# Two attention groups summed side by side in one PSUM bank, and turned once for both

## The chip, the cores and the metric

The kernel runs on one core of a Trainium2 chip. The metric is the device time of one execution in microseconds (us). The engines are TensorE (PE in the rows, its weight loads PEld), VectorE (DVE), ScalarE (ACT), GpSimd (POOL) and SyncE (SP), which issues most DMAs.

## The reference

One "macaron" layer on x of shape (8, 512, 128), all in float32: half a step of a feed-forward part that holds an attention of its own and a mixture of 8 experts, then an attention with rotary positions and 4 key and value heads, then the feed-forward part again. Both attentions have 16 heads of 8 elements.

```python
def _msa(x, w_qkv, w_proj):                      # 512 tokens of a batch as 4 x 128 here
    attn = softmax(q @ k.T / sqrt(8)); y = attn @ v; return y @ w_proj
def _L0_ffn_ref(x, ...):
    x = x + _msa(_layernorm(x, ln1_w, ln1_b), w_qkv, w_proj)
    return x + _moe_mlp(_layernorm(x, ln2_w, ln2_b), gate_w, gate_b, w1, w2)   # best expert of 8 per token
x = x + 0.5 * _L0_ffn_ref(_layernorm(x), ...)
x = x + _L0_attn_ref(_layernorm(x), w_q, w_k, w_v, w_o)
x = x + 0.5 * _L0_ffn_ref(_layernorm(x), ...)
```

The abridged lines leave out shapes. In the kernel each of the 8 batches of 512 tokens attends within itself.

## The kernel before

**Stages.** The program is two streams of attention, each followed by blocks of experts. Stream 0 (label 0) takes the 8 batches of the first feed-forward part. Stream 1 (label 1) takes 16: 8 of the middle attention and 8 of the second feed-forward part. A batch has 16 heads, worked on in G = 4 groups of J = 4 heads. So there are 32 groups in stream 0 and 64 in stream 1, 96 in all; n counts them within a stream.

**One group.** Group n takes four steps, kt = 0 to 3, one for each 128 keys. In a step TensorE computes the scores of 4 heads against 128 keys with all 512 queries (`score`, L839), ScalarE writes their exponentials to SBUF (L1181, four tiles of 128x512 per step), and TensorE multiplies them with the values (`weigh`, L851), one step later. Softmax needs a maximum for each query beforehand: in the same step TensorE also computes scores the other way round for group n + 2 (`max_score`, L823, four of 64x512), and VectorE reduces each two of them to maxima (`take_max`, L1210, two per step). The maxima of a group are split in two parts (L1218, L1220), turned (`turn_max`, L830), copied (L1232) and sent by DMA into rows of Q.

A step has two halves on TensorE. Each half is two matmuls of L823, two of L839 and eight of L851 (four heads, each float32 matmul as two instructions). `weigh` gives each head its own 32 partitions of bank 7: rows 32j to 32j + 8 hold 8 sums of values and, from a column of ones in V, the sum of the exponentials (V1 = 9).

**After a group.** ScalarE copies the whole bank 7 to the tile outT (`copy_out`, L1038) in step (n + 1, 0). TensorE turns it with four 128x128 transposes (`turn_out`, L860) in the list of step (n + 1, 2). VectorE takes the reciprocal of 16 sums per token (L1242) and multiplies (L1245) into the rows N (`normalise`).

**The ring.** L823 and everything else that isn't scores or weighted sums (rows of maxima, turned outputs, projections, values, gates) write to a ring of four PSUM banks. A use of the ring takes as many slots as it has banks; `put` rounds a list of a step up to an even number by making the last entry two slots wide. A slot can be used again when its consumer, VectorE or ScalarE, has released the use four slots back (`bank_for`). The lists stand in `Plan.group`: at kt = 0 the rows of maxima, at kt = 2 the turned output, and with either what `Plan.slot` adds. At kt = 2 that is q for n = 0 modulo 4, v for 2, proj for 3 and, for 1, k (middle attention), gate (feed-forward) or nothing. Of the 48 steps (n, 2) with odd n, 22 have "out" and proj, 12 "out" and gate, 6 "out" and k, and 8 "out" alone (n = 1, 3, 5 of stream 0; n = 3, 25, 29, 33, 37 of stream 1).

**Other places.** The tile V holds three slots of values; `copy_v` (L1071, L1075) fills one per batch, 24 in all. The tile `empty` holds zero rows with token numbers that name spare rows of `by_token`; eight of its entries are written behind each expert's tokens (`write_tails`), the other eight as two loads of 8 x 128 rows at the end of `sorted_x`. `later_loads` is a list of which SyncE issues one per group in stream 0.

Of the kernel before, what the change touches and what calls it, by code (L numbers as in the profile page):

```python
# [21 lines left out]
U32 = mybir.dt.uint32  # L22
# [4 lines left out]
P = 128  # L27
# [20 lines left out]
VCOLS = G * QT * J * V1  # L48
# [129 lines left out]
def setup(nc, c, a):  # L178
    with ExitStack() as ctx:
# [18 lines left out]
        def _(pool):  # L198
# [10 lines left out]
            nc.gpsimd.iota(c.empty[:, :, D].bitcast(U32), pattern=[[P, 2 * E]], base=NT * P, channel_multiplier=1)  # L209
# [37 lines left out]
def later_loads(c, a):  # L247

    loads = [(c.w1[:, e * HID:(e + 1) * HID], a["w1"][e]) for e in range(E)]
    loads += [(cols(c.w2, e * HID, HID).rearrange("p (k n) -> p k n", k=HT), a["w2"][e].rearrange("(k p) n -> p k n", p=P))  # L250
              for e in range(E)]
    loads += [
        (c.sorted_x[(E + (E + 1) * half) * REGION:(E + (E + 1) * half) * REGION + E * P, :].rearrange("(u p) w -> p u w", p=P),
         c.empty[:, E:2 * E, :]) for half in range(HALVES)]
    loads += [
        (c.wqk_mid[:, :], a["w_qk_mid"]), (c.wqk_rot[:, :], a["w_qk_rot"]),
        (c.wv[:, :], a["w_v"]), (c.wo[:, :], a["w_o"]),
        (c.cos[:, :], a["cos"]), (c.sin[:, :], a["sin"]),
    ]
    return loads  # L260

# [15 lines left out]
class Plan:  # L277
# [108 lines left out]
def stream(nc, c, ctx, a, label, kinds, past, blocks):  # L386
# [6 lines left out]
    if True:  # L393
# [7 lines left out]
        v4 = c.V[:, :].rearrange("p (b k g j e) -> p b k g j e", b=VSLOTS, k=QT, g=G, j=J)  # L401
# [151 lines left out]
        def write_tails(eng, half, experts):  # L553

            eng.wait_ge(s.tabled, half + 1)
            for expert in experts:
# [5 lines left out]
        def sync(sp):  # L562
# [60 lines left out]
            def main():  # L623
# [4 lines left out]
                for n in range(last):  # L628
# [33 lines left out]
        def gpsimd(pool):  # L662
# [145 lines left out]
        def tensor(pe):  # L808
# [47 lines left out]
            def turn_out(n):  # L856
                bank = bank_for("out", n)
                pe.wait_ge(s.out_copied, n + 1)
# [170 lines left out]
        def scalar(act):  # L1029
# [4 lines left out]
            def copy_out(n):  # L1034
                act.wait_ge(s.pv, 4 * n + 4)
                if n:
                    filled(act, "out", n - 1)
# [28 lines left out]
            def copy_v(b, bank):  # L1066
# [3 lines left out]
                if plan.ffn(b):  # L1070
                    ins = nc.scalar.activation(v.rearrange("p (h e) -> p h e", e=V1)[:, :, 0:HD],  # L1071
                                               bank.rearrange("p (h d) -> p h d", d=HD), ACT.Copy)
                else:
                    h = QT * G
                    ins = nc.scalar.activation(v.rearrange("p (h j e) -> p h j e", h=h, j=J)[:, :, :, 0:HD],  # L1075
                                               bank[:, 0:h * HD].rearrange("p (h j d) -> p h j d", h=h, j=1)
                                               .broadcast_to((P, h, J, HD)), ACT.Copy)
# [88 lines left out]
            def main():  # L1166
# [8 lines left out]
                for n in range(last):  # L1175
                    for kt in range(QT):
# [6 lines left out]
                        if kt == 0 and n:  # L1183
# [14 lines left out]
        def vector(dve):  # L1198
# [39 lines left out]
            def normalise(n):  # L1238
                filled(dve, "out", n)
                turned = ring[turns["out", n].first % RING].rearrange("p (t j r) -> p t j r", t=QT, j=J)  # L1240
                rec = cols(c.recip, n % 2 * QT * J, QT * J).rearrange("p (t j) -> p t j", t=QT)
                nc.vector.reciprocal(rec, turned[:, :, :, HD]).then_inc(s.recip, 1)  # L1242
                dve.wait_ge(s.recip, n + 1)
                dst = outputs(n // G).rearrange("p t (g j d) -> p t g j d", g=G, j=J)[:, :, n % G, :, :]
                freed(nc.vector.tensor_tensor(dst, turned[:, :, :, 0:HD],  # L1245
                                              rec.rearrange("p t (j o) -> p t j o", o=1).broadcast_to((P, QT, J, HD)),
                                              ALU.mult), "out", n)
# [429 lines left out]
def build(nc, a, out):  # L1677
    with ExitStack() as ctx:
# [9 lines left out]
        c.rest, c.zeroed = ctx.enter_context(nc.semaphore("rest")), ctx.enter_context(nc.semaphore("zeroed"))  # L1688
        c.X, c.Y, c.N = sb("X", [P, B * S]), sb("Y", [P, B * S]), sb("N", [P, NT * W])
# [20 lines left out]
        c.recip = sb("recip", [P, 2 * QT * J])  # L1710
        c.logits, c.onehot, c.rank = sb("logits", [P, 2 * QT * E]), sb("onehot", [P, 2 * QT * E]), sb("rank", [P, 2 * RANKS])
        c.before, c.empty, c.temp = sb("before", [P, HALVES * (HT_ROWS + 1) * E]), sb("empty", [P, 2 * E, W]), [sb(f"temp{i}", [P, 100]) for i in range(2)]
# [108 lines left out]
```

## Time and profile before

| | us |
|---|---|
| median of three runs | 1563.21 |
| lowest and highest run | 1561.63, 1566.58 |
| the profiled execution | 1566.45 |
| its span, first to last instruction | 1564.7 |
| TensorE busy | 1406.8 |
| VectorE busy | 1185.5 |
| ScalarE busy | 1124.5 |

The profiled execution has 1.75 us around its span. Its stretches: stream 0 attends from about 66 to 467 us and stream 1 from about 631 to 1436 us; the rest is the opening and the experts. Busy shares are those of whole stretches; what waits for what is read from the timeline of one group.

### The profile page before, as it was taken

The page shows a single profiled execution, that of the slowest core. Times are in us where ns is not written, and L with a number is a line of the kernel's source. Part 1 is how long each engine was busy: PE and PEld are TensorE (multiplying, and loading weights), DVE is VectorE, ACT ScalarE, POOL GpSimd, SP SyncE. Part 2 cuts the span into 40 slices and gives each one's busy share as a digit, 9 for nine tenths or more (in the row PEclk, how much of TensorE's full clock was granted, in tenths as well). Part 3 has the DMA queues.
Part 4 walks back from the last instruction along what each step waited for, and adds up shares of the span by engine and source line. Part 5 has one row for each costly group of instructions (what it writes and reads, how often), then busy time and mean ns, then how long its engine had stood idle before and what let it go on. Part 6 is the DMA issues. An engine that isn't in the chain of part 4 may idle for free.

```text
span 1564.7 us, 35538 instructions
## 1 busy us (share of the span) xinstructions
PE 1406.8 (90%) x12228; PEld 687.4 (44%) x12228; DVE 1185.5 (76%) x1945; ACT 1124.5 (72%) x2148; POOL 639.8 (41%) x972
## 2 busy tenths in 40 slices
PE   2899999999999886999999999999999999999895
PEld 1333334333339773333333333333334343334885
DVE  5788888888855254888888888888888888894532
ACT  1478887788785452778888887888887878787553
POOL 2422344542226555333544453233324543213753
PEclk8699999999999986999999999999999999999998
DMA  4344333533102315323322333332333233211243
GB/s 119 95 111 114 103 100 108 132 94 95 47 26 60 105 49 154 96 77 93 94 80 68 98 95 101 93 82 67 93 94 82 73 99 99 60 38 37 72 113 104
DMA packets 101423, 137.60 MB, mean 88 GB/s; under 512 B 29664, under 2 KB 72032, under 8 KB 101248
## 3 DMA queue, kind: packets, MB, share of 16 engines
q1 hardware_dynamic: 70864, 85.82, 19.1%
q0 software_dynamic: 24000, 45.04, 12.0%
q10 hardware_dynamic: 6384, 4.47, 1.0%
q8 instruction: 102, 1.67, 0.4%
q14 instruction: 73, 0.60, 0.1%
HBM read 79.05 MB, written 53.51 MB: 85 GB/s over the span
## 4 chain that ended last, share of the span: by engine, by line
PE 55%; DVE 31%; issue 6%; POOL 2%; DMA 2%; SPq 2%; ACT 1%; DVEq 0%; ACTq 0%; POOLq 0%
DVE maxima L1210 26%; PE banks L851 14%; PE banks L839 11%; PE banks L823 11%; PE banks L878 3%; PE banks L1554 3%; PE banks L860 3%; PE banks L1563 3%; PE banks L904 1%; PE banks L885 1%; SPq L463 1%; POOL by_token L1537 1%; DVE stats L1287 1%; DVE split L1218 1%; POOL sorted_x L691 1%
## 5 line engine op out<-in xcount | busy, mean ns | idle before, releaser
L1210 DVE TENSOR_REDUCE maxima<-banks 128x2 f32<-128x1024 f32 x768 | 924.2, 1222 | 171.9 <-PE banks L823 166.8
L1181 ACT ACTIVATE work<-banks 128x512 f32<-128x512 f32 x1536 | 829.3, 597 | 149.2 <-PE banks L839 135.2
L823 PE MATMUL banks<-K,Q 64*128 64x512 f32 x1536 | 572.7, 463 | 56.3 <-DVE maxima L1210 36.4
L839 PE MATMUL banks<-Q,K 64*128 64x512 f32 x1536 | 567.7, 451 | 0.6
L851 PE MATMUL banks<-work,V 128*9 128x256 f32 x6144 | 476.8, 382 | 1.6 <-ACT work L1181 0.8
L823 PEld LDWEIGHTS banks<-K,Q 64*128 64x128 f32 x1536 | 229.9, 190 | 214.6 <-DVE maxima L1210 126.4
L839 PEld LDWEIGHTS banks<-Q,K 64*128 64x128 f32 x1536 | 229.3, 186 | 181.7 <-issue 137.4
L851 PEld LDWEIGHTS banks<-work,V 128*9 128x9 f32 x6144 | 91.5, 88 | 276.1 <-issue 204.5
L710 POOL TENSOR_TENSOR lo<-full,hi 128x512 fp32r<-128x512 f32 x42 | 53.7, 1278 | 251.7 <-ACT hi L1059 144.4
L1617 DVE COPY work<-w 128x512 f32 x88 | 43.7, 497 | 87.2 <-PE banks L1554 75.5
L1563 PE MATMUL banks<-w,work 128*128 x736 | 102.3, 284 | 2.5 <-issue 1.3
L1537 POOL DMA_INDIRECT by_token<-work x76 | 76.2, 1003 | 66.2 <-ACT work L1597 55.6
L1554 PE MATMUL banks<-work 128*128 128x128 f32 x704 | 97.6, 284 | 0.6 <-DVE work L1617 0.6
L1563 PEld LDWEIGHTS banks<-w,work 128*128 128x128 f32 x736 | 94.3, 200 | 3.4 <-issue 3.3
L1554 PEld LDWEIGHTS banks<-work 128*128 128x128 f32 x704 | 89.9, 200 | 3.3 <-issue 2.0
L138 POOL TENSOR_SCALAR root<-moments 128x4 f32<-128x4 f32 x38 | 8.9, 233 | 196.8 <-DVE moments L1294 158.6
L1592 ACT ACTIVATE work<-banks 128x512 f32<-128x512 f32 x92 | 54.8, 596 | 30.6 <-PE banks L1554 30.5
L691 POOL DMA_INDIRECT sorted_x<-N,pos x64 | 65.2, 1019 | 19.9 <-issue 11.0
L860 PE MATMUL banks<-ident,outT 128*128 128x128 f32 x384 | 62.8, 286 | 6.2 <-DVE maxima L1210 4.6
L1057 ACT ACTIVATE full<-banks 128x512 f32<-128x512 f32 x46 | 27.5, 597 | 52.7 <-PE banks L878 51.9
L542 POOL TENSOR_TENSOR full<-full,cos_sb 128x512 f32<-128x512 f32 x12 | 15.4, 1286 | 119.9 <-ACT swap L1053 119.8
L1587 ACT ACTIVATE work<-banks,ln 128x128 f32<-128x128 f32 x92 | 41.8, 455 | 31.1 <-PE banks L1547 24.7
(187 smaller groups left out, 1331.8 us busy)
## 6 DMA issues: line engine op xcount, KB each, us to landing
Q<-q_scratch SPq DMA_DIRECT2D x188, 128.0 KB, 2.6
K<-k_scratch SPq DMA_DIRECT2D x376, 64.0 KB, 2.4
Q<-zero_rows SPq DMA_DIRECT2D x182, 64.0 KB, 2.2
q_scratch<-hi POOLq DMA_DIRECT2D x42, 256.0 KB, 4.7
q_scratch<-lo POOLq DMA_DIRECT2D x42, 256.0 KB, 6.8
k_scratch<-hi POOLq DMA_DIRECT2D x21, 256.0 KB, 4.6
k_scratch<-lo POOLq DMA_DIRECT2D x21, 256.0 KB, 6.8
work<-sorted_x SPq DMA_DIRECT2D x76, 66.0 KB, 1.9
```

The lines of the kernel that those rows point to most:

```text
L691: nc.gpsimd.indirect_dma_start(c.sorted_x[:, :], bass.IndirectOffsetOnAxis(ap=c.pos[:, t:t + 1], axis=0), c.rows[:, t, :], None).then_inc( ...
L710: nc.gpsimd.tensor_tensor(lo(b)[i].bitcast(F32R), full(b)[i], hi(b)[i], ALU.subtract).then_inc(s.lo[i], 1)
L823: fill(nc.tensor.matmul(bank, q4[parts(j), n % SLOTS, j // 2, qt * P:(qt + 1) * P], k4[parts(j), n % SLOTS, j // 2, :], start=True, stop=T ...
L839: nc.tensor.matmul(scp[x % EXPS][:, :], k4[parts(j), n % SLOTS, j // 2, kt * P:(kt + 1) * P], q4[parts(j), n % SLOTS, j // 2, :], start=Tr ...
L851: ins = nc.tensor.matmul(outp[32 * j:32 * j + V1, q], v4[:, n // G % VSLOTS, kt, n % G, j, :], prob[:, kt, j, q], start=(kt == 0 and half ...
L860: ins = nc.tensor.transpose(bank[:, t * P:(t + 1) * P], c.outT[:, t * P:(t + 1) * P], c.ident[:, :])
L1181: nc.scalar.activation(prob[:, kt, j ^ 1, :], scp[x % EXPS][:, :], ACT.Exp, scale=SCALE).then_inc(s.probs, 1)
L1210: nc.vector.tensor_reduce(c.maxima[:, at:at + 9:8], c.banks[:, k * S:(k + 2) * S].rearrange("p (m n) -> p m n", m=2), AX.X, ALU.max).then_ ...
L1537: nc.gpsimd.indirect_dma_start(c.by_token[:, :], bass.IndirectOffsetOnAxis(ap=x_sb(i)[:, D:D + 1].bitcast(U32), axis=0), y_sb[i % ring], N ...
L1554: ins = nc.tensor.matmul(hp[i % 2][:, t * P:(t + 1) * P], w1(i)[:, t * P:(t + 1) * P], uT[i % 2], start=True, stop=True)
L1563: ins = nc.tensor.matmul(yp, h[i % 2][:, t * P:(t + 1) * P], cols(c.w2, at + t * D, D), start=(t == 0), stop=(t == HT - 1))
L1592: nc.scalar.activation(h[i % 2], hp[i % 2][:, :], ACT.Gelu_apprx_tanh).then_inc(s.gelu, 1)
```

## The change

The results of an even group n and the odd group n + 1 now lie side by side in the same 32 partitions of bank 7. V gets 27 columns per pair and head: 9 of the even group (8 values and a one), 9 zeros, 9 of the odd group. An even group's weights are columns 0 to 17, an odd group's columns 9 to 26, so each `weigh` matmul has 18 stationary columns for 9, and each adds zeros to the other group's sums. The accumulation starts at the even group's first matmul and stops at the odd group's last. `copy_out`, `turn_out` and `normalise` run once per pair, for "out" of odd n alone; `normalise` takes one reciprocal of 32 sums and makes two multiplications. `copy_v` becomes two activations of half the size.

For room, `empty` is halved: first it holds the names for the two large spare loads, which SyncE issues together at n = 1 (`spare_rows`); at n = 8 GpSimd waits for them and writes the other names, for which `write_tails` waits.

```diff
@@ VCOLS
-VCOLS = G * QT * J * V1
+VPAIR = 3 * V1
+VCOLS = QT * G // 2 * J * VPAIR
@@ setup
-            nc.gpsimd.iota(c.empty[:, :, D].bitcast(U32), pattern=[[P, 2 * E]], base=NT * P, channel_multiplier=1)
+            nc.gpsimd.iota(c.empty[:, :, D].bitcast(U32), pattern=[[P, E]], base=NT * P + E * P, channel_multiplier=1)
@@ Plan.group
-        if kt == 2 and 1 <= n <= self.last:
+        if kt == 2 and 2 <= n <= self.last and n % 2 == 0:
             names += [("out", n - 1)]
@@ sync main
+                    if n == 1 and later:
+                        spare_rows(sp, c)
@@ gpsimd opening
-                    nc.gpsimd.memset(c.V[:, :], 1.0).then_inc(c.v_clear, 1)
+                    link(nc.gpsimd.memset(c.V[:, :], 1.0))
+                    nc.gpsimd.memset(c.V[:, :].rearrange("p (x e) -> p x e", e=VPAIR)[:, :, V1:2 * V1], 0.0).then_inc(c.v_clear, 1)
@@ gpsimd main
+                    if label == 0 and n == 2 * G:
+                        pool.wait_ge(c.spare, 16 * HALVES)
+                        nc.gpsimd.iota(c.empty[:, :, D].bitcast(U32), pattern=[[P, E]], base=NT * P, channel_multiplier=1)\
+                            .then_inc(c.renamed, 1)
@@ weigh
-                    if kt == 0:
-                        wait(pe, s.out_copied, n)
+                    if kt == 0 and n % 2 == 0:
+                        wait(pe, s.out_copied, n // 2)
...
+                odd = n % 2
                 for j in range(J):
-                    ins = nc.tensor.matmul(outp[32 * j:32 * j + V1, q], v4[:, n // G % VSLOTS, kt, n % G, j, :], prob[:, kt, j, q],
-                                           start=(kt == 0 and half == 0), stop=(kt == QT - 1 and half == 1))
+                    ins = nc.tensor.matmul(outp[32 * j:32 * j + 2 * V1, q],
+                                           v4[:, n // G % VSLOTS, kt, n % G // 2, j, V1 * odd:V1 * odd + 2 * V1], prob[:, kt, j, q],
+                                           start=(n % 2 == 0 and kt == 0 and half == 0), stop=(n % 2 == 1 and kt == QT - 1 and half == 1))
@@ scalar: copy_v, main
+                pairs_of = v.rearrange("p (h j e) -> p h j e", h=QT * G // 2, j=J)
+                for odd in range(2):
+                    dst = pairs_of[:, :, :, 2 * V1 * odd:2 * V1 * odd + HD]
...
+                    ins = nc.scalar.activation(dst, src, ACT.Copy)
...
-                        if kt == 0 and n:
+                        if kt == 0 and n and n % 2 == 0:
                             copy_out(n - 1)
@@ normalise
-                nc.vector.reciprocal(rec, turned[:, :, :, HD]).then_inc(s.recip, 1)
+                nc.vector.reciprocal(rec, turned[:, :, :, HD:2 * V1:V1]).then_inc(s.recip, 1)
...
+                for odd in range(2):
+                    ins = nc.vector.tensor_tensor(dst[:, :, n % G - 1 + odd, :, :], turned[:, :, :, V1 * odd:V1 * odd + HD],
+                                                  rec[:, :, :, odd:odd + 1].broadcast_to((P, QT, J, HD)), ALU.mult)
```

On TensorE, step (7, 2) of stream 0, the first with proj, reads so before (work is the tile of exponentials; a count behind x is of heads or tiles):

```order
L839 MATMUL banks<-Q,K 128x512
L823 MATMUL banks<-K,Q 128x512
L851 MATMUL banks<-work,V 9x256 x4
L860 MATMUL banks<-ident,outT 128x128 x4
L904 MATMUL banks<-wproj,turned 128x128 x4
L823 MATMUL banks<-K,Q 128x512
L839 MATMUL banks<-Q,K 128x512
```

and so after the change, with the new file's line numbers (L836 and L852 for L823 and L839, L865 for L851, L919 for L904):

```order
L852 MATMUL banks<-Q,K 128x512
L836 MATMUL banks<-K,Q 128x512
L865 MATMUL banks<-work,V 18x256 x4
L919 MATMUL banks<-wproj,turned 128x128 x4
L836 MATMUL banks<-K,Q 128x512
L852 MATMUL banks<-Q,K 128x512
```

The four transposes are gone from this odd step, proj keeps its place, and the stationary operand of the weighted sums has 18 columns. In steps (n, 2) with even n the transposes stay.

On VectorE, steps (7, 2) and (8, 2) of stream 0 read so before:

```order
L1210 TENSOR_REDUCE maxima<-banks 128x2 x2
L1242 RECIPROCAL recip<-banks 128x16
L1245 TENSOR_TENSOR N<-banks,recip 128x4x32
L1210 TENSOR_REDUCE maxima<-banks 128x2 x2
...
L1210 TENSOR_REDUCE maxima<-banks 128x2 x2
L1242 RECIPROCAL recip<-banks 128x16
L1245 TENSOR_TENSOR N<-banks,recip 128x4x32
L1210 TENSOR_REDUCE maxima<-banks 128x2 x2
L1218 CAST split<-maxima 128x2x8
```

and step (8, 2) so after:

```order
L1226 TENSOR_REDUCE maxima<-banks 128x2 x2
L1258 RECIPROCAL recip<-banks 128x32
L1262 TENSOR_TENSOR N<-banks,recip 128x4x32 x2
L1226 TENSOR_REDUCE maxima<-banks 128x2 x2
L1234 CAST split<-maxima 128x2x8
```

The odd step has no reciprocal and no multiplication any more; the even step has one more multiplication.

## Rows read from the trace of the kernel before

**Rows 1.** The page's first part: busy time, share of the span, instructions of each engine.

```profile
PE 1406.8 (90%) x12228; PEld 687.4 (44%) x12228; DVE 1185.5 (76%) x1945; ACT 1124.5 (72%) x2148; POOL 639.8 (41%) x972
```

**Rows 2.** Stream 1's stretch: busy PE, PEld, DVE, ACT, POOL; granted clock, DMA share, GB/s.

```profile
640.00:1435.00 795.00, 756.84 (x6844) 303.90 (x6842) 674.79 (x1010) 646.25 (x1201) 311.05 (x475) 1.00 0.31 82
```

**Rows 3.** Timeline of TensorE at an odd step with proj: start and duration in us.

```profile
1229.98 0.62 PE L851 MATMUL banks<-work,V 128*9 128x256 f32 x8
...
1231.19 0.62 PE L851 MATMUL banks<-work,V 128*9 128x256 f32 x8
1231.74 0.66 PE L860 MATMUL banks<-ident,outT 128*128 128x128 f32 x4
1232.24 1.06 PE L904 MATMUL banks<-wproj,turned 128*128 128x128 f32 x8
...
1233.88 0.62 PE L851 MATMUL banks<-work,V 128*9 128x256 f32 x8
```

**Rows 4.** Timeline of VectorE over the same step; in brackets its idle time before.

```profile
1230.23 2.40 DVE L1210 TENSOR_REDUCE maxima<-banks 128x2 f32<-128x1024 f32 x2
...
1234.06 2.48 DVE L1210 TENSOR_REDUCE maxima<-banks 128x2 f32<-128x1024 f32 x2 [0.94 <-PE banks L823]
```

**Rows 5.** Timeline of TensorE at an odd step whose list is "out" alone.

```profile
1001.50 0.62 PE L851 MATMUL banks<-work,V 128*9 128x256 f32 x8
1002.05 0.66 PE L860 MATMUL banks<-ident,outT 128*128 128x128 f32 x4
1003.00 0.49 PE L823 MATMUL banks<-K,Q 64*128 64x512 f32 x1 [0.28 <-DVE maxima L1210]
...
1003.66 0.62 PE L851 MATMUL banks<-work,V 128*9 128x256 f32 x8
```

**Rows 6.** Timeline of VectorE over that same step.

```profile
998.05 4.89 DVE L1210 TENSOR_REDUCE maxima<-banks 128x2 f32<-128x1024 f32 x4 [0.71 <-PE banks L823]
1002.86 0.25 DVE L1242 RECIPROCAL recip<-banks 128x16 f32<-128x16 f32 x1
1003.21 0.29 DVE L1245 TENSOR_TENSOR N<-banks,recip 128x128 f32<-128x128 f32 x1
1003.84 2.47 DVE L1210 TENSOR_REDUCE maxima<-banks 128x2 f32<-128x1024 f32 x2 [0.34 <-PE banks L823]
```

**Rows 7.** Timeline of TensorE at a kt = 0 step with rows of maxima.

```profile
1225.86 0.27 PE L830 MATMUL banks<-ident,split 128*32 128x128 f32 x1 [0.88 <-DVE maxima L1210]
```

**Rows 8.** Timeline of weight loads at another odd step with proj.

```profile
314.13 0.12 PEld L851 LDWEIGHTS banks<-work,V 128*9 128x9 f32 x8 [0.36 <-issue]
314.68 0.42 PEld L860 LDWEIGHTS banks<-ident,outT 128*128 128x128 f32 x4 [0.43 <-DVE maxima L1210]
315.07 0.97 PEld L904 LDWEIGHTS banks<-wproj,turned 128*128 128x128 f32 x8
```

**Rows 9.** Timeline of VectorE at two even steps, ahead of kt = 3.

```profile
1220.90 2.47 DVE L1210 TENSOR_REDUCE maxima<-banks 128x2 f32<-128x1024 f32 x2 [0.55 <-PE banks L823]
...
1246.86 1.23 DVE L1210 TENSOR_REDUCE maxima<-banks 128x2 f32<-128x1024 f32 x1 [0.72 <-PE banks L823]
```

**Rows 10.** Groups by line: count, then busy us, mean ns of one, idle before.

```profile
L851 PEld LDWEIGHTS banks<-work,V 128*9 128x9 f32 x6144 | 91.5, 88 | 276.1 <-issue 204.5 <-ACT work L1181 71.2
...
L1597 ACT ACTIVATE work<-banks 128x128 f32<-128x128 f32 x92 | 25.5, 277 | 32.2 <-PE banks L1563 31.9
...
L830 PEld LDWEIGHTS banks<-ident,split 128*32 128x32 f32 x96 | 9.1, 95 | 75.7 <-issue 70.9 <-DVE split L1220 4.8
...
L1071 ACT ACTIVATE V<-banks 128x512 f32<-128x512 f32 x16 | 9.6, 599 | 20.4 <-PE banks L885 19.7 <-issue 0.6
```

**Rows 11.** Timeline of the opening, GpSimd and VectorE.

```profile
1.33 1.86 POOL L205 MEMSET empty<- 128x2112 f32 x1
...
7.11 2.95 DVE L1402 TENSOR_SCALAR root<-moments 128x4 f32<-128x4 f32 x1
9.97 1.56 POOL L730 MEMSET V<- 128x1728 f32 x1
```

More of the change, by code:

```diff
@@ L252, in later_loads @@
     loads += [
-        (c.sorted_x[(E + (E + 1) * half) * REGION:(E + (E + 1) * half) * REGION + E * P, :].rearrange("(u p) w -> p u w", p=P),
-         c.empty[:, E:2 * E, :]) for half in range(HALVES)]
-    loads += [
         (c.wqk_mid[:, :], a["w_qk_mid"]), (c.wqk_rot[:, :], a["w_qk_rot"]),
@@ L260, in later_loads, with spare_rows @@
     return loads
+def spare_rows(sp, c):
+    for half in range(HALVES):
+        at = (E + (E + 1) * half) * REGION
+        sp.dma_start(c.sorted_x[at:at + E * P, :].rearrange("(u p) w -> p u w", p=P), c.empty[:, :, :]).then_inc(c.spare, 16)
 def load_outputs(eng, c, b):
@@ L555, in write_tails @@
             eng.wait_ge(s.tabled, half + 1)
+            eng.wait_ge(c.renamed, 1)
             for expert in experts:
@@ L857, in turn_out @@
                 bank = bank_for("out", n)
-                pe.wait_ge(s.out_copied, n + 1)
+                pe.wait_ge(s.out_copied, n // 2 + 1)
                 for t in range(QT):
@@ L1035, in copy_out @@
                 act.wait_ge(s.pv, 4 * n + 4)
-                if n:
-                    filled(act, "out", n - 1)
+                if n > 1:
+                    filled(act, "out", n - 2)
                 nc.scalar.activation(c.outT[:, :], outp[:, :], ACT.Copy).then_inc(s.out_copied, 1)
@@ L1069, in copy_v @@
                 v = cols(c.V, b % VSLOTS * VCOLS, VCOLS)
[L1070 to L1077, printed above, removed]
+                pairs_of = v.rearrange("p (h j e) -> p h j e", h=QT * G // 2, j=J)
+                for odd in range(2):
+                    dst = pairs_of[:, :, :, 2 * V1 * odd:2 * V1 * odd + HD]
+                    if plan.ffn(b):
+                        src = bank.rearrange("p (h o j d) -> p h o j d", o=2, j=J, d=HD)[:, :, odd, :, :]
+                    else:
+                        src = bank[:, 0:QT * G * HD].rearrange("p (h o j d) -> p h o j d", o=2, j=1, d=HD)[:, :, odd, :, :]\
+                            .broadcast_to((P, QT * G // 2, J, HD))
+                    ins = nc.scalar.activation(dst, src, ACT.Copy)
                 evacuated(ins, "v", b)
@@ L1240, in normalise @@
                 turned = ring[turns["out", n].first % RING].rearrange("p (t j r) -> p t j r", t=QT, j=J)
-                rec = cols(c.recip, n % 2 * QT * J, QT * J).rearrange("p (t j) -> p t j", t=QT)
-                nc.vector.reciprocal(rec, turned[:, :, :, HD]).then_inc(s.recip, 1)
[L1243 to L1247, printed above, removed]
+                rec = cols(c.recip, n // 2 % 2 * 2 * QT * J, 2 * QT * J).rearrange("p (t j o) -> p t j o", t=QT, j=J)
+                nc.vector.reciprocal(rec, turned[:, :, :, HD:2 * V1:V1]).then_inc(s.recip, 1)
+                dve.wait_ge(s.recip, n // 2 + 1)
+                dst = outputs(n // G).rearrange("p t (g j d) -> p t g j d", g=G, j=J)
+                for odd in range(2):
+                    ins = nc.vector.tensor_tensor(dst[:, :, n % G - 1 + odd, :, :], turned[:, :, :, V1 * odd:V1 * odd + HD],
+                                                  rec[:, :, :, odd:odd + 1].broadcast_to((P, QT, J, HD)), ALU.mult)
+                freed(ins, "out", n)
             def add_gate_bias(f):
@@ L1688, in build @@
         c.rest, c.zeroed = ctx.enter_context(nc.semaphore("rest")), ctx.enter_context(nc.semaphore("zeroed"))
+        c.spare, c.renamed = ctx.enter_context(nc.semaphore("spare")), ctx.enter_context(nc.semaphore("renamed"))
         c.X, c.Y, c.N = sb("X", [P, B * S]), sb("Y", [P, B * S]), sb("N", [P, NT * W])
@@ L1709, in build @@
         c.warm = sb("warm", [P, 1])
-        c.recip = sb("recip", [P, 2 * QT * J])
+        c.recip = sb("recip", [P, 4 * QT * J])
         c.logits, c.onehot, c.rank = sb("logits", [P, 2 * QT * E]), sb("onehot", [P, 2 * QT * E]), sb("rank", [P, 2 * RANKS])
-        c.before, c.empty, c.temp = sb("before", [P, HALVES * (HT_ROWS + 1) * E]), sb("empty", [P, 2 * E, W]), [sb(f"temp{i}", [P, 100]) for i in range(2)]
+        c.before, c.empty, c.temp = sb("before", [P, HALVES * (HT_ROWS + 1) * E]), sb("empty", [P, E, W]), [sb(f"temp{i}", [P, 100]) for i in range(2)]
         c.pos, c.expert_at, c.row_at = sb("pos", [P, NT], U32), sb("expert_at", [1, HALVES * NBLK], U32), sb("row_at", [1, HALVES * NBLK], U32)
```

2 lines of the change are left out of this document (1 added, 1 removed).

## The prediction

> **What bounds the kernel now.** I read the page first, for who is busy: TensorE 90% of the span, VectorE 76%, ScalarE 72% [rows 1]. In stream 1's stretch TensorE is busy 756.84 of 795 us at a granted clock of 1.00, that is 2.4 GHz, VectorE 674.79 [rows 2]. Shares so close don't tell who sets the time, so I read the timelines of single steps.
>
> In the odd step with proj, the eight `weigh` matmuls of one half start at 1229.98 and those of the next at 1231.19: a half-step is 1.21 us when nothing stands between. The next start is 1233.88, so the transposes and proj stretch 1.21 to 2.69 us [rows 3]. Over this place VectorE ends its reductions at 1230.23 + 2.40 = 1232.63, normalises, and then sits idle 0.94 us until TensorE has filled two banks [rows 4]. TensorE's own work sets the time here.
>
> In the odd step with "out" alone, the `weigh` starts lie 2.16 us apart (1001.50 to 1003.66), and TensorE restarts at 1003.00 after an idle wait for VectorE [rows 5]. The four reductions of kt = 1 and 2 end at 998.05 + 4.89 = 1002.94; at once TensorE restarts [rows 6]. So with the ring's two slots taken by "out", the next L823 needs the banks of the last reduction: this step is closed by VectorE, and then VectorE waits 0.34 us for the fill. The two engines stop for each other once at kt = 2 and once at kt = 0, where TensorE waits 0.88 us for a reduction before it can turn the maxima [rows 7]. Between these places (kt = 1 to 2, and kt = 3 to 0) VectorE reduces without a gap.
>
> **The change part by part.**
>
> *Transposes, 40 odd steps with another entry (22 proj, 12 gate, 6 k).* The loads of the four transposes start at 314.68 and proj's at 315.07 [rows 8]: 0.39 us by which all behind comes earlier. Is TensorE still the one waited for? It began its next pair about 0.66 us (1003.66 - 1003.00, from rows 5) before the `weigh` at 1233.88, at 1233.22; 0.39 earlier is 1232.83, still behind the end of the reductions at 1232.63 [rows 4]. VectorE also loses its 0.25 + 0.29 us of reciprocal and multiplication [rows 6], so it waits at least as before. 40 x 0.39 = 15.6 us. The most a step with proj could give before VectorE closes it is 2.69 - 2.16 = 0.53 us.
>
> *The 8 odd steps with "out" alone.* Here the two ring slots go as well. TensorE can run on at 1002.05, and has the next two banks filled 0.84 us later (1003.00 to 1003.84 is that delay), at 1002.89. VectorE, without normalising, is free at 1002.94 rather than restarting at 1003.84 [rows 5, 6]: 0.90 us each, 7.2 us.
>
> *The even steps.* TensorE does what it did. VectorE has a second multiplication, 0.29 us [rows 6] and some 0.04 of gap. It is covered by the idle time ahead of the reduction of kt = 3, which is 0.55 us in the step with v (behind statistics too) and 0.72 with q [rows 9]. Zero; without this cover it would be 48 x 0.33 = 16 us. The reciprocal of 32 for 16 I take as no longer.
>
> *ScalarE's 48 copies of bank 7 fall away.* They stand in steps where TensorE waits for VectorE [rows 7], so I give them nothing. Nobody else is queued on them: an odd group's `weigh` no longer waits for a copy, but it did not wait before either, with the start-to-start at 1.21.
>
> *Eighteen columns for nine.* No row shows this load. The eight loads of a half take 0.12 us together, though one takes 88 ns [rows 8, 10], so they start within about 32 ns of each other and overlap. From below: a load of 32 columns takes 95 ns [rows 10], that is (95 - 88)/23 = 0.3 ns per column, 2.7 ns for nine. From above: four loads of 128 columns take 0.42 us [rows 8], 105 ns each, 0.82 ns per column, or 7.4 ns for nine; if all eight were paid one behind another, 59 ns in a half-step. I take one load of 7.4 ns exposed per half-step, since the eight overlap in the row. It counts only where TensorE is the one waited for: four of a group's eight half-steps (kt = 1 and 2; from kt = 3 to kt = 0 TensorE has the 0.88 us to spare), 384 in all: 384 x 0.0074 = 2.8 us. The stream of 256 queries is unchanged.
>
> The Trainium skill, "TensorE: Matmul & The Clock Gate", section "LDWEIGHTS (loading the stationary operand)", puts a load at columns / 1.2 ns, here 7.5 ns more, and its Part 3 says that loads overlap running matmuls only in another row group; all eight here use the same 128 rows. Taken together that would make eight loads of nine columns 60 ns end to end, where the row shows starts within about 32 ns, so it is only partly borne out; by it the sum would lose about 23 us, which is the rival below.
>
> *Values.* 24 copies of 599 ns become pairs of 256 elements each; between 277 ns for 128 elements and 599 for 512 [rows 10] that is 0.38 each, 0.17 us more per batch. ScalarE begins its exponentials later by that; a part may reach TensorE through the score banks. Bounds are 0 and 24 x 0.17 = 4.1; I take 1.0.
>
> *Opening.* Half of the 1.86 us memset of `empty` goes, so all behind the setup comes 0.93 earlier. The memset of V, 1.56 us, becomes 2.34 and gets a second one of half the size, 0.78. VectorE's L1402 took 2.95 us and ended at 10.06, when the next GpSimd memset had begun [rows 11]; a later one of its kind could now be held in the same way for up to about 0.8 us. Together zero, within 0.9 either way.
>
> *Spare rows.* Two loads move to n = 1, ahead of SyncE's weight load, and one wait and one iota enter GpSimd's queue at n = 8. Behind SyncE's issues stand the maxima's rows for a group a whole group's time ahead, and behind GpSimd's wait the k and q of a batch two groups ahead. Zero; 1 us at most.
>
> **Sum.** -15.6 - 7.2 + 2.8 + 1.0 = -19.0 us on the profiled execution's 1566.45, so 1547.4. That execution was 3.2 us above the median of three, 1563.21; against the median it is 1544.2, which I forecast as 1544.
>
> **Rivals.**
>
> *Weight loads eat the gain (1563).* If the eight loads follow one another, each of the 384 half-steps grows by 59 ns: 22.7 us against 22.8 saved, and 1 for V. For it: all eight share their rows, and loads of 128 columns do start 105 ns apart. Against it: eight loads fit in 0.12 us. The TensorE page of the skill speaks for this one, as said.
>
> *Loads are paid in every half-step, slower (1586).* The same 59 ns, but with no cover at kt = 3 and 0 either: 768 x 0.059 = 45.3 us, less 22.8, is +22.5. It decides from 22.8/768 = 30 ns per half-step on, if each one pays. Against it: 4 x 0.059 = 0.24 us is less than the 0.88 us that TensorE waits there [rows 7].
>
> *VectorE takes over (1554).* If something late on VectorE (choices of experts, statistics) closes the odd steps, half of each 0.39 is lost, 7.8 us, and perhaps 2 of the even steps' multiplications: about -9. For it: only 0.20 us lie between 1232.63 and 1232.83. Against it: it has 0.94 us idle afterwards.
>
> *More gain (1534).* The drained start of proj may hide less than 0.39 suggests: with 0.53 in each of the 40, and no price for loads or values, 21.2 + 7.2 = 28.4 us.
>
> **How the numbers follow.** My forecast (between 1537 and 1551) 0.66; weight loads eat the gain, in whole or in large part (1552 to 1565) 0.13; VectorE takes over 0.09; more gain 0.06; slower 0.06. The range reaches from 1536, inside the larger gain, to 1558, inside the weight-load case, leaving about 2 in 10 outside. A measurement of this kernel tells about 0.3%, 4.7 us, from no change. Faster: forecast, larger gain, VectorE case and some of the weight-load case, 0.85; the same 0.09; slower 0.06.
>
> **What would show it.** Transposes, copies of bank 7 and reciprocals must be 192, 48 and 48. The odd step with proj should go from 2.69 to about 2.31 us between `weigh` starts, the lone one from 2.16 to about 1.22. A plain half-step tells the weight load: 1.21 to 1.22 by me, 1.27 by the rival. VectorE's idle time ahead of kt = 3 should fall to about 0.2 and 0.4 us in even steps, and stay above zero. If the half-step is 1.22 and the time still doesn't fall, the gain went to VectorE, which would show as TensorE idle for L1210 in the odd steps with proj.

## The result, and the profile after

The changed kernel takes 1546.47 us (median of four runs, 1546.29 to 1549.42) against 1562.55 of the kernel before (four runs): the ratio is 0.9893, 95% interval 0.9875 to 0.9911. The forecast was 1544 us, range 1536 to 1558. In a later comparison (the run again below), where the kernel before took 1577.32 us, the ratio was 0.9887 (0.9864 to 0.9910). The profiled execution went from 1566.45 to 1546.33 us, 20.1 us less, against 19.0 worked out for it.

The page's first part for the changed kernel [of before: rows 1]:

```profile
PE 1391.6 (90%) x12036; PEld 680.1 (44%) x12036; DVE 1177.6 (76%) x1897; ACT 1102.3 (71%) x2124; POOL 640.9 (41%) x974
```

TensorE has 192 matmuls and VectorE 48 instructions fewer; the shares stay within a point of what they were. In stream 1's stretch, now 622 to 1414 us [rows 2]; the columns are busy us of TensorE, its weight loads, VectorE, ScalarE and GpSimd, then the granted clock, DMA share and GB/s:

```profile
622.00:1414.00 792.00, 756.55 (x6800) 302.61 (x6796) 677.73 (x988) 637.51 (x1196) 311.76 (x476) 1.00 0.32 84
```

The clock is 2.4 GHz (1.00) in both. The odd step with proj on TensorE [rows 3], here of group 51 (line numbers are the new file's: L865 weighs, L919 is proj, L836 the scores for maxima):

```profile
1260.68 0.63 PE L865 MATMUL banks<-work,V 128*18 128x256 f32 x8
...
1261.90 0.63 PE L865 MATMUL banks<-work,V 128*18 128x256 f32 x8
...
1263.12 0.63 PE L865 MATMUL banks<-work,V 128*18 128x256 f32 x8
1263.67 1.16 PE L919 MATMUL banks<-wproj,turned 128*128 128x128 f32 x8
...
1265.42 0.63 PE L865 MATMUL banks<-work,V 128*18 128x256 f32 x8
```

Half-steps are 1.22 us now, and from 1263.12 to 1265.42 it takes 2.30 us where it took 2.69. VectorE in the same step [rows 4]:

```profile
1262.13 2.43 DVE L1226 TENSOR_REDUCE maxima<-banks 128x2 f32<-128x1024 f32 x2
1265.60 1.23 DVE L1226 TENSOR_REDUCE maxima<-banks 128x2 f32<-128x1024 f32 x1 [1.05 <-PE banks L836]
```

Its idle time has grown from 0.94 to 1.05 us: TensorE is still the one waited for. A step with "out" alone before, now with an empty list (group 29) [rows 5]:

```profile
982.84 0.63 PE L865 MATMUL banks<-work,V 128*18 128x256 f32 x8
...
984.06 0.63 PE L865 MATMUL banks<-work,V 128*18 128x256 f32 x8
...
985.28 0.63 PE L865 MATMUL banks<-work,V 128*18 128x256 f32 x8
...
986.50 0.63 PE L865 MATMUL banks<-work,V 128*18 128x256 f32 x8
987.06 0.50 PE L836 MATMUL banks<-K,Q 64*128 64x512 f32 x1
...
987.72 0.63 PE L865 MATMUL banks<-work,V 128*18 128x256 f32 x8
```

Nothing stands between the half-steps any more: 986.50 to 987.72 is 1.22 us for 2.16. VectorE [rows 6]:

```profile
983.01 7.36 DVE L1226 TENSOR_REDUCE maxima<-banks 128x2 f32<-128x1024 f32 x6 [0.71 <-PE banks L836]
```

Six reductions follow each other where there were four, a pause and two. In an even step VectorE has the longer normalisation ahead of kt = 3 [rows 9]:

```profile
1199.86 0.35 DVE L1258 RECIPROCAL recip<-banks 128x32 f32<-128x32 f32 x1
1200.24 0.49 DVE L1262 TENSOR_TENSOR N<-banks,recip 128x128 f32<-128x128 f32 x2
1200.65 0.48 DVE L1304 BATCH_NORM_STATS2 stats<-X 128x6 f32<-128x128 f32 x2
1201.39 2.48 DVE L1226 TENSOR_REDUCE maxima<-banks 128x2 f32<-128x1024 f32 x2 [0.27 <-PE banks L836]
```

Idle time fell from 0.55 to 0.27 us and hides it. The groups by line: count, busy us, mean ns of one, idle before [rows 10]:

```profile
L865 PEld LDWEIGHTS banks<-work,V 128*18 128x18 f32 x6144 | 103.5, 96 | 275.2 <-issue 200.5 <-ACT work L1197 74.3
...
L875 PE MATMUL banks<-ident,outT 128*128 128x128 f32 x192 | 31.3, 286 | 5.9 <-DVE maxima L1226 4.3 <-ACT outT L1053 1.6
L1053 ACT ACTIVATE outT<-banks 128x512 f32<-128x512 f32 x48 | 29.1, 606 | 2.4 <-PE banks L865 2.4
...
L1258 DVE RECIPROCAL recip<-banks 128x32 f32<-128x32 f32 x48 | 16.7, 348 | 12.2 <-PE banks L875 12.2
...
L1093 ACT ACTIVATE V<-banks 128x256 f32<-128x256 f32 x48 | 16.4, 400 | 27.6 <-PE banks L900 27.6
```

192 transposes, 48 copies of the bank and 48 reciprocals, as the change says. The reciprocal of 32 takes 348 ns, where that of 16 took 247 (0.25 in the timeline [rows 6]). A value copy takes 400 ns.

**Where the time went.** The attention stretches can be taken out of the trace by the first and last half-step of `weigh` of each stream. Each row is worked out from four start times of one profiled execution.

| kernel | first `weigh` at | stream 0 | between | stream 1 | rest | both streams |
|---|---|---|---|---|---|---|
| before | 66.7 | 400.1 | 164.4 | 804.8 | 128.7 | 1204.9 |
| changed | 65.3 | 392.2 | 164.2 | 792.1 | 130.8 | 1184.3 |
| changed, later comparison | 66.0 | 394.4 | 168.1 | 793.7 | 134.5 | 1188.1 |

The gain lies in the streams, 20.6 us. What lies between and behind them is the experts, whose length differs by some us from one profiled execution to the next (158.0 to 164.4 us between the streams in the traces of before, changed and experiments 1, 2, 3 and 5), whether changed or not. The changed kernel and its three variants of experiment 5 show it: their spans lie 5.9 us apart (1538.7 to 1544.6 us), their streams 1.6 (1183.7 to 1185.3). So below both are given: the ratio of all runs, and the sum of the two streams in the trace.

The start times of all 768 half-steps tell more. From the kernel before to the changed one, the 40 odd steps with another entry are 15.3 us shorter in all and the 8 lone ones 7.5 us. Of the other half-steps 13 differ by over 0.1 us each, together by -1.0 (0.9 of it at the very first); all the rest, which differ by less than that, are 3.1 us longer in sum. That is the price of the wider loads as the streams show it, and no further cost stands out.

### The profile page after: what moved, and what is told of

Its sections match the earlier page's. It is cut to its first block, busy times and chain, and to the rows that moved or that the text cites. A ratio compares the mean times of both kernels' runs of the same rounds, so it can differ in the third digit from the quotient of the medians.

```text
span 1544.6 us, 34941 instructions
## 1 busy us (share of the span) xinstructions
PE 1391.6 (90%) x12036; PEld 680.1 (44%) x12036; DVE 1177.6 (76%) x1897; ACT 1102.3 (71%) x2124; POOL 640.9 (41%) x974
## 4 chain that ended last, share of the span: by engine, by line
PE 57%; DVE 27%; issue 7%; DMA 3%; SPq 2%; POOL 2%; ACT 1%; DVEq 0%; ACTq 0%; POOLq 0%
DVE maxima L1226 23%; PE banks L865 16%; PE banks L852 12%; PE banks L836 11%; PE banks L893 4%; PE banks L1571 3%; PE banks L1580 3%; PE banks L875 2%; PE banks L919 2%; PE banks L900 1%; SPq L468 1%; POOL by_token L1554 1%; PE banks L935 1%; DVE stats L1304 1%; POOL sorted_x L699 1%
## 5 line engine op out<-in xcount | busy, mean ns | idle before, releaser
L836 PE MATMUL banks<-K,Q 64*128 64x512 f32 x1536 | 571.8, 463 | 51.2 <-DVE maxima L1226 34.4
L852 PE MATMUL banks<-Q,K 64*128 64x512 f32 x1536 | 567.3, 451 | 0.5
L865 PE MATMUL banks<-work,V 128*18 128x256 f32 x6144 | 482.3, 386 | 1.5 <-ACT work L1197 0.8
L836 PEld LDWEIGHTS banks<-K,Q 64*128 64x128 f32 x1536 | 229.6, 190 | 209.4 <-DVE maxima L1226 130.8
L852 PEld LDWEIGHTS banks<-Q,K 64*128 64x128 f32 x1536 | 229.3, 186 | 178.0 <-ACT work L1197 132.1
L865 PEld LDWEIGHTS banks<-work,V 128*18 128x18 f32 x6144 | 103.5, 96 | 275.2 <-issue 200.5
L1554 POOL DMA_INDIRECT by_token<-work x76 | 76.9, 1012 | 67.7 <-ACT work L1614 57.4
L140 POOL TENSOR_TENSOR rstd<-root,minus_half 128x4 f32<-128x4 f32 x52 | 54.1, 1040 | 4.4
```

The lines of the kernel that those rows point to most:

```text
L140: link(eng.tensor_tensor(out, half, c.minus_half[:, :], ALU.pow))
L836: fill(nc.tensor.matmul(bank, q4[parts(j), n % SLOTS, j // 2, qt * P:(qt + 1) * P], k4[parts(j), n % SLOTS, j // 2, :], start=True, stop=T ...
L852: nc.tensor.matmul(scp[x % EXPS][:, :], k4[parts(j), n % SLOTS, j // 2, kt * P:(kt + 1) * P], q4[parts(j), n % SLOTS, j // 2, :], start=Tr ...
L865: ins = nc.tensor.matmul(outp[32 * j:32 * j + 2 * V1, q], v4[:, n // G % VSLOTS, kt, n % G // 2, j, V1 * odd:V1 * odd + 2 * V1], prob[:, k ...
L1554: nc.gpsimd.indirect_dma_start(c.by_token[:, :], bass.IndirectOffsetOnAxis(ap=x_sb(i)[:, D:D + 1].bitcast(U32), axis=0), y_sb[i % ring], N ...
```

## The experiments

Every ratio is taken against the kernel before, run beside it. "Both streams" is the sum of the two attention stretches in one trace, as above.

**1. Wider loads alone (w18, w28).** The kernel before, with 18 or 28 columns in each weighted sum; the extra sums are never read. WIDE is 18 or 28.

```diff
+VSTRIDE = VCOLS + WIDE - V1
...
-                    ins = nc.tensor.matmul(outp[32 * j:32 * j + V1, q], v4[:, n // G % VSLOTS, kt, n % G, j, :], prob[:, kt, j, q],
+                    at = n // G % VSLOTS * VSTRIDE + ((kt * G + n % G) * J + j) * V1
+                    ins = nc.tensor.matmul(outp[32 * j:32 * j + WIDE, q], c.V[:, at:at + WIDE], prob[:, kt, j, q],
```

> The kernel before, with 18 stationary columns in each weighted-sum matmul (the nine columns of the next head are taken along; their sums are never read) and nothing else changed. In the trace of the changed kernel a plain half-step went from 1.21 to 1.22 us. Theory: only the four half-steps per group pay in which TensorE is the one waited for: 384 x 0.009 = about +3.3 us on the kernel before. Rival: every half-step pays, 768 x 0.009 = +6.7 us. Rival of the prediction, eight loads one behind another: half-steps of 1.27 us and +23 us or more.

> The same with 28 columns, as a larger dose: 19 more than nine. If a half-step grows in proportion to the columns, by about 0.95 ns for each, it is 1.23 us. Theory (four of eight half-steps pay): +7 us on the kernel before. Rival (all pay): +14 us. If the load's price is a fixed step and not per column, it is the same as with 18 columns.

With 18 columns: ratio 1.0015 (1.0002 to 1.0028), both streams 1209.3 us, 4.4 more. With 28: ratio 1.0046 (1.0030 to 1.0061), 1212.5 us, 7.6 more. The timeline of TensorE with 28 columns, at kt = 1 and 2 of group 29:

```profile
1002.34 0.64 PE L853 MATMUL banks<-work,V 128*28 128x256 f32 x8
...
1003.57 0.64 PE L853 MATMUL banks<-work,V 128*28 128x256 f32 x8
...
1004.79 0.64 PE L853 MATMUL banks<-work,V 128*28 128x256 f32 x8
...
1006.02 0.64 PE L853 MATMUL banks<-work,V 128*28 128x256 f32 x8
```

and the group of its loads:

```profile
L853 PEld LDWEIGHTS banks<-work,V 128*28 128x28 f32 x6144 | 116.6, 105 | 275.9 <-issue 204.8 <-ACT work L1183 70.7
```

Three half-steps of a run last 3.63 us with nine columns (997.87 to 1001.50, of which rows 5 show the last), 3.66 with 18 (982.84 to 986.50 above), and 3.68 with 28 (1002.34 to 1006.02). Over all plain half-steps the mean is 1.212, 1.221 (1.220 in the changed kernel) and 1.229 us, so 0.9 ns for each added column: it goes by columns and is paid about once per half-step, not eight times. A half-step of 1.27 us is ruled out. That not all of them are on the path is shown by 28 columns: 1.0046 is 7.2 us, interval 4.7 to 9.5, where 384 x 0.017 = 6.5 and 768 x 0.017 = 13. With 18 columns, 2.4 us (0.3 to 4.4) fits 384 x 0.0085 = 3.3 and leaves out 6.5.

The streams' 4.4 and 7.6 look like more than half. But 1.5 of the 4.4 stands at one place, group 3 of stream 0, and 1.4 of the 7.6 at nine single half-steps that differ by over 0.1 us each. Without these the streams are 2.9 and 6.1 us longer, close to 384 half-steps in both. Every plain half-step grows, and those with TensorE's wait for VectorE at kt = 0 shrink, by 1.8 us in all with 18 columns and 3.5 with 28: there the covered part is given back.

The measured 0.9 ns is near the 0.82 per column at which loads of 128 columns follow each other [rows 8]. The Trainium skill, "TensorE: Matmul & The Clock Gate", section "LDWEIGHTS (loading the stationary operand)", has columns / 1.2 ns for a load, 0.83 ns per column. The measured 0.9 agrees with one such load exposed per half-step. In Part 3 of that page the Trainium skill says that loads overlap running matmuls only in another row group; read as "loads of the same rows follow one another", this does not describe these eight.

**2. Pairing without wider loads (narrow).** The odd group's sums are added onto the even group's rows and both multiplications read that place, so the output is not the layer's.

```diff
-                    ins = nc.tensor.matmul(outp[32 * j:32 * j + 2 * V1, q],
-                                           v4[:, n // G % VSLOTS, kt, n % G // 2, j, V1 * odd:V1 * odd + 2 * V1], prob[:, kt, j, q],
+                    ins = nc.tensor.matmul(outp[32 * j:32 * j + V1, q],
+                                           v4[:, n // G % VSLOTS, kt, n % G // 2, j, 2 * V1 * odd:2 * V1 * odd + V1], prob[:, kt, j, q],
...
-                nc.vector.reciprocal(rec, turned[:, :, :, HD:2 * V1:V1]).then_inc(s.recip, 1)
+                nc.vector.reciprocal(rec, turned[:, :, :, HD:HD + 1].broadcast_to((P, QT, J, 2))).then_inc(s.recip, 1)
```

> The changed kernel with nine stationary columns again: the odd group's sums are added onto the even group's in the same rows and both multiplications read that one place as before, so the output is not the reference's. It shows what pairing gives without the wider loads. Theory: about 3.3 us under the changed kernel, near 20 us under the kernel before, with half-steps of 1.21 us. Rival (all half-steps pay): 6.7 us under the changed kernel.

Ratio 0.9851 (0.9833 to 0.9868), 1540.64 us; both streams 1182.5 us, 1.8 less than the changed kernel's. By the ratio it is 0.0042 or 6.6 us less against the first comparison of the changed kernel, and 5.6 against the later one, whose interval overlaps. So this run doesn't tell 3.3 from 6.7; the half-steps are 1.212 us again.

**3. The ring slots of the lone steps (hold).** In the eight odd steps whose list the change emptied, two slots are taken by one small transpose.

```diff
+        if kt == 2 and 1 <= n < self.last and not names:
+            names += [("hold", n)]
...
+                bank = bank_for("hold", n)
+                fill(nc.tensor.transpose(bank[0:32, 0:P], c.ident[:, 0:32], c.ident[:, :]), "hold", n)
...
+                        freed(nc.vector.tensor_copy(c.held[:, :], ring[turns["hold", i].first % RING][0:32, 0:4]), "hold", i)
```

> The changed kernel, but in the steps kt = 2 whose list is now empty (the eight lone odd steps) two ring slots are taken up by one small transpose of 32 columns and a tiny copy on VectorE. Theory: the slots, not the four transposes, closed these steps: the start-to-start of the weighted sums goes back from 1.22 to about 2.15 us, and the time is some 7 us above the changed kernel. Rival: the transposes' own time was the cost; then the small one costs about 0.1 to 0.3 us each, 1 to 2 us in all.

Ratio 0.9922 (0.9903 to 0.9940); both streams 1192.7 us, 8.4 more than the changed kernel's, 7.5 of it in the eight steps themselves. TensorE at group 29:

```profile
988.60 0.63 PE L867 MATMUL banks<-work,V 128*18 128x256 f32 x8
989.15 0.29 PE L882 MATMUL banks<-ident 128*32 128x128 f32 x1
990.09 0.50 PE L838 MATMUL banks<-K,Q 64*128 64x512 f32 x1 [0.65 <-DVE held L1295]
...
990.75 0.63 PE L867 MATMUL banks<-work,V 128*18 128x256 f32 x8
```

VectorE at the same place:

```profile
985.11 4.92 DVE L1234 TENSOR_REDUCE maxima<-banks 128x2 f32<-128x1024 f32 x4 [0.71 <-PE banks L838]
989.95 0.14 DVE L1295 COPY held<-banks 32x4 f32<-32x4 f32 x1
990.93 1.23 DVE L1234 TENSOR_REDUCE maxima<-banks 128x2 f32<-128x1024 f32 x1 [0.84 <-PE banks L838]
```

One transpose of 0.29 us in place of four, and the `weigh` starts are 2.15 us apart again (988.60 to 990.75), because TensorE waits 0.65 us for VectorE: its four reductions end at 985.11 + 4.92 = 990.03. The slots closed these steps, as forecast; the transposes' length there didn't matter.

**4. TensorE's work put back in all 48 odd steps (peback).** VectorE's and ScalarE's part of the saving stays.

```diff
+        if kt == 2 and 1 <= n < self.last and n % 2:
+            names += [("hold", n)]
...
+                for t in range(QT):
+                    ins = nc.tensor.transpose(bank[:, t * P:(t + 1) * P], c.ident[:, :], c.ident[:, :])
+                fill(ins, "hold", n)
```

> The changed kernel with TensorE's work and the ring slots of the odd steps put back: four transposes of the identity in each of 48 odd steps kt = 2, and a tiny copy on VectorE that releases the bank. VectorE's reciprocals and multiplications, and ScalarE's copies, stay away. Theory: all of the gain was TensorE's 0.39 us in 40 steps and the closing of 8; so the attention stretches go back to those of the kernel before with 18 columns (1209 us), and the time is about 1.001 of the kernel before. Rival: what VectorE and ScalarE no longer do is part of the gain; then the time stays some us under the kernel before.

Ratio 1.0051 (1.0035 to 1.0067). Both streams 1211.3 us, 23.2 more than the changed kernel's in the same comparison (1188.1), where 22.8 were forecast for the odd steps. The step with proj on TensorE:

```profile
1241.24 0.63 PE L867 MATMUL banks<-work,V 128*18 128x256 f32 x8
1241.80 0.66 PE L883 MATMUL banks<-ident 128*128 128x128 f32 x4
1242.29 1.06 PE L927 MATMUL banks<-wproj,turned 128*128 128x128 f32 x8
...
1243.94 0.63 PE L867 MATMUL banks<-work,V 128*18 128x256 f32 x8
```

It is 2.70 us long again. The 40 steps give back 15.6 us and the 8 lone ones 7.5; all other half-steps together differ by 0.1. So no part of the gain in the streams is left for VectorE's or ScalarE's saving.

The total missed what was expected: about 1.001, where the interval starts at 1.0035. Of the 26.8 us between the profiled executions of peback and the changed kernel beside it, 3.6 lie outside the streams, most of it between and behind them, where this edit adds nothing. The ratio is 0.0036 (5.6 us) above that of w18, whose TensorE does the same in the streams; that kernel ran in the earlier comparison, and its streams are 2.0 us shorter. What makes the rest was not settled.

**5. Engines beside the path (mul3, copies, setup).** One more multiplication per normalisation, 46 copies of 128x512 back on ScalarE (the expectation counts 47; the first odd group of each stream has none), and GpSimd's memset at its old length.

```diff
+                    if odd == 0:
+                        nc.vector.tensor_tensor(c.spill[:, :].rearrange("p (t j d) -> p t j d", t=QT, j=J), turned[:, :, :, 0:HD],
+                                                rec[:, :, :, 0:1].broadcast_to((P, QT, J, HD)), ALU.mult)
```

```diff
+                        if kt == 0 and n % 2 and n > 1:
+                            act.wait_ge(s.pv, 4 * n)
+                            act.wait_ge(s.out_copied, n // 2)
+                            filled(act, "out", n - 2)
+                            nc.scalar.activation(c.outT[:, :], c.outT[:, :], ACT.Copy).then_inc(s.idled, 1)
```

```diff
             nc.gpsimd.memset(c.empty[:, :, :], 0.0)
+            nc.gpsimd.memset(c.Y[:, 0:E * W], 0.0)
```

> The changed kernel with one more multiplication (128x128 into a tile that nobody reads) in each of the 48 normalisations, some 0.33 us of VectorE each. In the changed kernel VectorE is idle ahead of kt = 3 for about 0.43 to 0.62 us in steps with q, 0.18 to 0.27 in steps with v, 0.11 in the few with the output alone. Theory: the idle time covers it but for what is lacking in the steps with v and the lone ones: about +3 us on the changed kernel. Rival (VectorE sets the time of the even steps): 48 x 0.33 = +16 us. It also tells that the second multiplication of the change, which met more idle time, cost nothing.

> The changed kernel with a copy of 128x512 put back on ScalarE in 47 of the odd steps kt = 0 (outT onto itself, where the copy of the bank stood before). Theory: these copies lie beside a wait of TensorE for VectorE; the time is that of the changed kernel within 1 us. Rival: the copies were part of the gain; up to 47 x 0.6 = 28 us, and at least some us above the changed kernel.

> The changed kernel with the setup's memset on GpSimd at its old length (a second one of 1056 elements per partition on a tile that is written later anyway). Theory: the setup ends 0.9 us later and so do the first reductions, +0.9 us. Rival: the opening is bound by something else and nothing moves.

| kernel | ratio | interval | both streams |
|---|---|---|---|
| mul3 | 0.9876 | 0.9854 to 0.9898 | 1185.3 |
| copies | 0.9868 | 0.9845 to 0.9891 | 1185.0 |
| setup | 0.9887 | 0.9867 to 0.9908 | 1183.7 |

All three are the changed kernel's time (0.9893 and 0.9887) within their intervals. mul3 was expected at +3 and shows +1.0 in the streams, where copies shows +0.7 and setup -0.6: no more than such traces differ. VectorE in mul3's step with v:

```profile
1200.17 0.35 DVE L1258 RECIPROCAL recip<-banks 128x32 f32<-128x32 f32 x1
1200.55 0.29 DVE L1262 TENSOR_TENSOR N<-banks,recip 128x128 f32<-128x128 f32 x1
1200.76 0.28 DVE L1265 TENSOR_TENSOR spill<-banks,recip 128x128 f32<-128x128 f32 x1
1200.96 0.28 DVE L1262 TENSOR_TENSOR N<-banks,recip 128x128 f32<-128x128 f32 x1
1201.16 0.47 DVE L1307 BATCH_NORM_STATS2 stats<-X 128x6 f32<-128x128 f32 x2
1201.69 2.48 DVE L1226 TENSOR_REDUCE maxima<-banks 128x2 f32<-128x1024 f32 x2
```

The added multiplication starts only 0.21 us (1200.55 to 1200.76, 1200.96) after the one before, and so uses up the idle time and no more. The rivals, 16 us and 28 us, are ruled out. The setup's 0.9 us can't be told from the spread of the totals; the first `weigh` came at 67.2 rather than 65.3, but with mul3, whose opening is unchanged, it came at 67.7, so the opening itself varies by more. Its early part did move. VectorE's small L1420 in setup (L1419 in the changed kernel, whose rows stand further down):

```profile
7.13 2.95 DVE L1420 TENSOR_SCALAR root<-moments 128x4 f32<-128x4 f32 x1
...
12.48 0.74 DVE L1420 TENSOR_SCALAR root<-rstd 128x4 f32<-128x4 f32 x1
```

The second ends at 13.22 rather than 12.53, 0.69 us later. Whether that reaches the end of the program isn't shown.

**6. Nine columns where they do (mixed), and the changed kernel again.**

```diff
+                many = V1 if odd == 0 and kt else 2 * V1
                 for j in range(J):
-                    ins = nc.tensor.matmul(outp[32 * j:32 * j + 2 * V1, q],
-                                           v4[:, n // G % VSLOTS, kt, n % G // 2, j, V1 * odd:V1 * odd + 2 * V1], prob[:, kt, j, q],
+                    ins = nc.tensor.matmul(outp[32 * j:32 * j + many, q],
+                                           v4[:, n // G % VSLOTS, kt, n % G // 2, j, V1 * odd:V1 * odd + many], prob[:, kt, j, q],
```

> The changed kernel once more, on the chip and beside the runs that the next two are compared with. Theory: near 1546 us, 0.989 of the kernel before; the two attention stretches together near 1184.3 us in its trace, as in the first one, and what differs lies between the streams and at the end.

> The changed kernel with nine stationary columns in the even groups' matmuls of kt = 1 to 3, where the zeros add nothing that is needed; kt = 0 keeps 18, which writes the odd group's rows. Correct, and three of eight half-steps a pair have the narrow load. Theory: these half-steps fall from 1.220 to 1.212 us, some 1 to 2 us on the whole, under what a measurement tells; the trace shows it. Rival: changing the number of columns between matmuls costs something, and the half-steps don't fall or grow.

The changed kernel: 0.9887 (0.9864 to 0.9910), both streams 1188.1. mixed: 0.9869 (0.9845 to 0.9893), both streams 1186.2, 1.9 less. TensorE in mixed:

```profile
1002.77 0.63 PE L866 MATMUL banks<-work,V 128*18 128x256 f32 x8
...
1003.99 0.62 PE L866 MATMUL banks<-work,V 128*9 128x256 f32 x8
...
1005.20 0.62 PE L866 MATMUL banks<-work,V 128*9 128x256 f32 x8
```

The half-steps of even groups from kt = 1 on are 1.213 us on average, all others 1.220, so the saving is there, as expected, and no cost of changing the width shows. The intervals of the two ratios overlap: it may be the faster kernel by 1 to 2 us, and these runs don't show it as such.

## Why the prediction was right

**Transposes beside another entry, 40 x 0.39.** Right. Between `weigh` starts the step with proj takes 2.308 us (median of 22) for 2.690. These 0.38 us have 0.01 for the wider load in them, so the transposes were the forecast's 0.39. The forecast was 2.31. The steps with gate and k fell alike: all 40 lost 0.31 to 0.43 us, 0.38 on average, and against w18, which has the wider loads already, they are 15.6 us shorter in sum, the forecast's number.

**Eight lone steps, 8 x 0.90.** Right in size and in cause: 2.153 to 1.220 us, 7.5 us in all, and putting back the slots alone gave these 7.5 us again (hold).

**The two together.** 22.8 us forecast, 23.1 measured in the 48 steps by putting them back, 23.2 in the streams (peback).

**Wider loads, +2.8.** Right in mechanism, slightly small: 8.5 ns in w18 and 8 in the changed kernel for 7.4 per half-step, 3.1 to 3.3 us. Both halves of the reasoning held: one load exposed (1.220 us, not 1.27), and about half of the half-steps on the path (2.9 and 6.1 us in the streams of w18 and w28 without their single outliers, for 3.3 and 6.5).

**Even steps at zero.** Right, though I took the reciprocal of 32 for as long as that of 16, and it is 0.10 longer. Together with the second multiplication VectorE works 0.30 us longer (1199.86 to 1201.12 in the step with v above, 1219.39 to 1220.35 before), for 0.33 forecast. The idle time left is 0.27 with v; with q it is 0.42, where it was 0.72 [rows 9]:

```profile
1227.11 1.23 DVE L1226 TENSOR_REDUCE maxima<-banks 128x2 f32<-128x1024 f32 x1 [0.42 <-PE banks L836]
```

These are the "about 0.2 and 0.4" of the forecast. mul3 shows that there was still something left.

**ScalarE's copies at zero.** Right (copies: no slower with 46 of them back).

**Values, +1.0.** One copy takes 400 ns for 384 assumed. No run isolates them. The half-steps' 3.1 us are used up by the wider loads, so nothing near the other 1.0 us shows in the streams: this term was a guess between its bounds, and too large if anything.

**Opening, zero.** The mechanism came as described, with one correction: in the kernel before, L1402 ended at 10.06 together with GpSimd's memset of K (5.67 + 4.36 = 10.03), the one before the memset that the prediction names. The rows of the opening [rows 11], GpSimd's memsets and VectorE's L1419 (L1402 before):

```profile
1.33 0.98 POOL L206 MEMSET empty<- 128x1056 f32 x1
...
5.00 4.36 POOL L737 MEMSET K<- 128x5120 f32 x1 [1.34 <-POOLq L126]
...
7.32 2.06 DVE L1419 TENSOR_SCALAR root<-moments 128x4 f32<-128x4 f32 x1
...
9.30 2.28 POOL L738 MEMSET V<- 128x2592 f32 x1
...
11.64 0.86 POOL L739 MEMSET V<- 128x864 f32 x1
11.78 0.75 DVE L1419 TENSOR_SCALAR root<-rstd 128x4 f32<-128x4 f32 x1
```

The memset of `empty` is 0.88 us shorter, and the memset of K starts 0.67 earlier; with its end (9.36) ends the first L1419 (9.38). But the second L1419 takes 0.75 us, where it took 0.17 before, ending at 12.53 just after the last memset's end at 12.50. Before, it ended at 12.62: what the setup gave, that one took back but for 0.09 us.

**Spare rows, zero.** No run isolates them; no cost of them stands out in the streams.

**The sum.** -19.0 us forecast; 20.1 less in the profiled execution, 16.1 by the medians, 16.7 by the ratio (13.9 to 19.5), 17.8 by the second comparison. The profiled execution of the kernel before was among its slowest (1566.45 for a median of 1562.55), that of the changed kernel at its median. In the traces what differs from execution to execution lies mostly in the opening and the experts; for runs without a trace this isn't shown. That 20.1 came out so near 19.0 is in part luck: the streams alone gave 20.6, because the removals gave 0.3 more than forecast, the loads cost 0.5 more, single half-steps happened to be 1.0 shorter and the value copies' 1.0 was not seen; outside the streams 0.5 us went the other way.

**The rivals.** Loads one behind another in each of the eight: no, a half-step is 1.22 us. Loads paid in every half-step: no; even their 17 ns of w28 are not paid in all. VectorE taking over: no, it waits longer than before in the odd steps. More gain, up to 0.53 per step: no; the four transposes were worth their own 0.39.

## What to carry to other kernels

Price a removed piece of TensorE work at the place where it stood: the same four transposes were worth 0.39 us where another entry of the list came behind them, and 0.93 where they alone took two slots of the ring, because there the engines waited for each other. When two engines are both near 85 to 95% busy, look for the places at which each stops for the other; between them one engine is covered, so a small cost spread over all steps (here wider weight loads) is paid in part of them only. Four results side by side in 32-partition strips leave room for a second set at the cost of columns in the weight load, nearly free here: 0.9 ns per column and half-step.

## What the runs showed of the hardware

Eight weight loads for four column strips of TensorE overlap but for one: 9, 18 and 28 columns give half-steps of 1.212, 1.220 to 1.221 and 1.229 us: nine more columns cost 8 to 9 ns, where eight loads one behind another would have cost 59 (eight times 7.4, from the 0.82 ns per column of rows 8). A reciprocal on VectorE takes 247 ns for 16 and 348 ns for 32 elements per partition, 6.3 ns for each more, where a multiplication of 128 takes about 290. A small tensor-scalar instruction on VectorE (L1419, 0.17 us elsewhere in the trace) lasted 2.06 and 0.75 us while GpSimd was in a memset and ended within 0.03 us of it (9.38 for 9.36, 12.53 for 12.50).
